# Top-64 attention: two of the seven removals of found candidates go from VectorE to GpSimd, whose mask of a row is issued in six parts

## The reference, cut to what matters

```python
scores = einsum('bhqd,bhkd->bhqk', q, k) / scale       # [16 heads, 2048, 1601 or 2048]
top_scores, top_idx = jax.lax.top_k(scores, 64)
w = softmax(top_scores)                                # all other keys have weight 0
out = einsum('bhqk,bhqkd->bhqd', w, v gathered by top_idx)
```

## Time and profile before

| | us |
|---|---|
| median of 3 runs | 8678.82 (8678.73 to 8685.87) |
| the profiled execution: its own time | 8695.39 |
| its span, first to last instruction | 8693.6 |
| busy in the span: TensorE, VectorE, ScalarE, GpSimd | 6502.8, 6476.1, 4444.7, 3965.1 |

### The profile page before, as it was taken

The page is one execution under the profiler, slowest core; times in us unless marked ns, Lnnn a source line. Parts: engine busy times, 40 slices in busy tenths (PEclk is TensorE's granted clock), DMA queues, the critical chain, the costliest instruction groups (busy, mean ns, idle before and its releaser), DMA issues. The chain is left out here.

```text
span 8693.6 us, 157925 instructions
## 1 busy us (share of the span) xinstructions
PE 6502.8 (75%) x31114; PEld 2666.4 (31%) x31240; DVE 6476.1 (74%) x41675; ACT 4444.7 (51%) x8491; POOL 3965.1 (46%) x2643
## 2 busy tenths in 40 slices
PE   6998477774677767998566777776657899999974
PEld 3333222221222224665222232222223322222213
DVE  4664899999999994554799999999996444444424
ACT  1665466664666652112567777776655332323320
POOL 0001355553555541221456666665644065656650
PEclk7999666665666667999677777776767999999986
DMA  2000000000000000000000000000000411111122
GB/s 75 19 22 12 31 8 5 8 5 4 8 5 8 8 2 17 22 15 16 32 9 5 7 8 9 6 9 5 6 5 19 164 31 31 38 40 31 31 47 64
DMA packets 81575, 193.10 MB, mean 22 GB/s; under 512 B 23728, under 2 KB 38062, under 8 KB 77230
## 3 DMA queue, kind: packets, MB, share of 16 engines
q1 hardware_dynamic: 72366, 169.98, 7.0%
q10 hardware_dynamic: 8192, 12.59, 0.6%
HBM read 118.97 MB, written 62.76 MB: 21 GB/s over the span
## 5 line engine op out<-in xcount | busy, mean ns | idle before, releaser
L2152 DVE TENSOR_REDUCE l1xc_part_max<-l1xc_by_query 128x1 f32<-128x512 f32 (+1 forms) x1024 | 559.5, 571 | 753.3 <-PE l1xc_by_query L2011 731.4
L2110 ACT ACTIVATE l1xc_prob<-l1xc_less_max 128x512 f32<-128x512 f32 (+1 forms) x832 | 451.2, 594 | 1004.4 <-PE l1xc_less_max L2025 935.9
L582 PE MATMUL l1ac_by_query<-l1ac_k_stack,l1ac_q_stack 97*128 (+1 forms) x1024 | 423.0, 470 | 695.8 <-ACT keep_xT L677 364.2
L770 DVE MAX8 l1ac_cand<-l1ac_score 128x8 f32<-128x39 f32 (+1 forms) x6656 | 863.1, 192 | 31.8 <-ACT l1ac_score L677 17.0
L552 POOL TENSOR_SCALAR l1ac_lost<-l1ac_score,l1ac_tops 128x2048 bf16<-128x2048 f32 x128 | 696.0, 5437 | 411.4 <-DVE l1ac_tops L789 387.1
L582 PE MATMUL l0xc_by_query<-l0xc_k_stack,l0xc_q_stack 97*128 (+2 forms) x1024 | 375.1, 431 | 664.8 <-ACT keep_xT L677 448.7
L770 DVE MAX8 l1ac_cand<-keep_xT 128x8 f32<-128x39 f32 (+1 forms) x6656 | 863.0, 191 | 4.4
L1973 POOL TENSOR_TENSOR l1xc_total<-l1xc_total,l1xc_prob 128x2048 f32<-128x2048 f32 (+1 forms) x176 | 794.2, 4513 | 72.3 <-POOL l1xc_v_tile L1983 72.0
L770 DVE MAX8 l0xc_cand<-l0xc_score 128x8 f32<-128x31 f32 (+1 forms) x6656 | 800.9, 182 | 27.6 <-ACT l0xc_score L677 15.8
L552 POOL TENSOR_SCALAR l1ac_lost<-keep_xT,l1ac_tops 128x2048 bf16<-128x2048 f32 x128 | 696.3, 5440 | 244.4 <-DVE l1ac_tops L789 244.4
L770 DVE MAX8 l0xc_cand<-keep_xT 128x8 f32<-128x31 f32 (+1 forms) x6656 | 801.7, 182 | 4.4
(11 more groups left out here) (479 smaller groups left out, 14320.9 us busy)
## 6 DMA issues: line engine op xcount, KB each, us to landing
l1xc_k<-wide_k SPq DMA_DIRECT2D x32, 400.2 KB
moe_w<-in_L_ffn_mlp_w_dram SPq DMA_DIRECT2D x16, 512.0 KB, 4.2
wide_q<-l1xp_full SPq DMA_DIRECT2D x8, 1024.0 KB, 3.9
...
```

The source lines that it names most:

```text
L582: nc.tensor.matmul(sA[c % 2][:, 0:w], Qm[0:SHIFT_ROW, bass.ds(at + i * P, P)], Kb[0:SHIFT_ROW, bass.ds(at + a, w)], start=True, stop=True) ...
L770: seg = nc.vector.max(new[:, j:8 * NSEG:NSEG], score[i % 4][:, a:a + w])
L2110: nc.scalar.activation(prob[0:n, buf(j), c], yP[c % 2][0:n], ACT.Exp).then_inc(y_taken, 1)
L2152: nc.vector.tensor_reduce(part_max[:, i % 2, c:c + 1], a_bank(i, c)[:, 0:w], AX.X, ALU.max).then_inc(a_taken, 1)
```

## The change

VectorE's first two removals of a tile are dropped. In their place GpSimd runs two instructions each, in `remove`: TENSOR_SCALAR over 52 candidates (is it at least the eighth value found, times -3e38) into a new tile `gone`, and TENSOR_TENSOR, which adds `gone` to the candidates. VectorE's first two MAX8 count up `picked`, GpSimd waits for it, and VectorE's second and third MAX8 wait for `removed`. The 52 segment instructions are spread anew: 15 of them stand behind the first MAX8 and 15 behind the second (`GAP` is 9 places), and one or two behind each of the 11 steps that are left. GpSimd's mask is issued in six parts (267 or 342 keys each), of which one stands behind each removal and the rest behind `part_max` and `stage_v`. In slot s GpSimd removes from row tile s-2 while it masks row tile s-3.

```diff
--- before.py
+++ after.py
@@ -362,6 +362,8 @@
     SET = 3
     BEGIN = 7
     TURN = 3
+    POOLED = 2
+    MASK_PARTS = tiles_of(nk, (nk + 5) // 6)
     QUADS = [list(range(a, min(a + 4, NKT))) for a in range(0, 16, 4)]
     UNITS = QC * NKT
     DV = DH + 1
@@ -377,6 +379,7 @@
         cands = [s.sb(f"cand{b}", [P, 8 * NSEG]) for b in range(2)]
         tops = s.sb("tops", [P, 8, TOPK])
         top_full = s.sb("top_full", [P, TOPK])
+        gone = s.sb("gone", [P, NSEG])
         missed, missed2 = s.sb("missed", [P, 4]), s.sb("missed2", [P, 4])
         anyflag = s.sb("anyflag", [1, 4])
         less_exact = s.sb("less_exact", [P, 1])
...
@@ -546,22 +550,45 @@
                 hold(pool, (parted, at + 5))
                 nc.gpsimd.tensor_copy(stat_parts[:, 2], neg_rest[:, 1]).then_inc(parted, 1)
 
-            def mask(n, i, chunk):
-
-                hold(pool, (y_formed, NKT * (chunk - 1) + F_AHEAD))
-                nc.gpsimd.tensor_scalar(lost[:, i % 8, 0:nk], score[i % 4][:, 0:nk], tops[:, i % 8, TOPK - 1:TOPK], None,
-                                        ALU.is_lt).then_inc(masked, 1)
+            def mask(i, k):
+
+                a, w = MASK_PARTS[k]
+                part = nc.gpsimd.tensor_scalar(lost[:, i % 8, a:a + w], score[i % 4][:, a:a + w],
+                                               tops[:, i % 8, TOPK - 1:TOPK], None, ALU.is_lt)
+                if k == len(MASK_PARTS) - 1:
+                    part.then_inc(masked, 1)
+
+            def remove(n, i, r):
+
+                part = cands[i % 2][:, 0:UPTO[r]]
+                hold(pool, (picked, POOLED * n + r + 1))
+                nc.gpsimd.tensor_scalar(gone[:, 0:UPTO[r]], part, tops[:, i % 8, 8 * r + 7:8 * r + 8], -3.0e38,
+                                        ALU.is_ge, ALU.mult).then_inc(goes, 1)
+                hold(pool, (goes, POOLED * n + r + 1))
+                nc.gpsimd.tensor_tensor(part, part, gone[:, 0:UPTO[r]], ALU.add).then_inc(removed, 1)
+
+            def picks(h, i):
+
+                return (not (isinstance(h, int) and h == 0) or i >= 2) and not (isinstance(h, int) and h == H and i >= 2)
 
             def slot(h, i, searching, producing):
+                settling = settles(h, i)
+                it = (i - SET) % QT
+                ht = h if i >= SET else h - 1
+                todo = list(range(len(MASK_PARTS))) if settling else []
+                if settling:
+                    hold(pool, (extracted, h * QT + i - SET + 1), (y_formed, NKT * (4 * ht + it // 4 - 1) + F_AHEAD))
+                if picks(h, i):
+                    for r in range(POOLED):
+                        remove(h * QT + i - 2, (i - 2) % QT, r)
+                        for k in todo[r:r + 1]:
+                            mask(it, k)
+                if settling and it % 4 == 3:
+                    part_max(ht, it // 4)
                 if producing:
                     stage_v(*products_of(h, i))
-                if settles(h, i):
-                    n, it = h * QT + i - SET, (i - SET) % QT
-                    ht = h if i >= SET else h - 1
-                    hold(pool, (extracted, n + 1))
-                    if it % 4 == 3:
-                        part_max(ht, it // 4)
-                    mask(n, it, 4 * ht + it // 4)
+                for k in todo[POOLED if picks(h, i) else 0:]:
+                    mask(it, k)
 
             pool.sem_inc(masked, S_AHEAD)
             slots(pool, slot)
@@ -759,7 +786,8 @@
                 top = tops[:, (i - 1) % 8]
                 count, other = chains[i % 2], chains[(i + 1) % 2]
                 first = isinstance(n, int) and n == 0
-                SLICES = 2 * ROUNDS + 1
+                GAP = 9
+                SLICES = 2 * ROUNDS + 1 + POOLED * (GAP - 2)
                 searching = not (isinstance(n, int) and n == H * QT)
 
                 def some_segments(r):
@@ -780,21 +808,36 @@
                 dve.wait_ge(count, 1)
                 some_segments(0)
                 at = 1
+                place = 1
                 for r in range(2 * ROUNDS - 1):
                     some = top[:, 8 * (r // 2):8 * (r // 2) + 8]
                     part = old[:, 0:UPTO[r // 2]]
+                    last = r == 2 * ROUNDS - 2
+                    if r < 2 * POOLED:
+                        if r % 2 == 0:
+                            if r:
+                                hold(dve, (removed, POOLED * (n - 1) + r // 2))
+                            else:
+                                dve.wait_ge(count, at)
+                            nc.vector.max(some, part).then_inc(picked, 1)
+                            for _ in range(GAP):
+                                some_segments(place)
+                                place += 1
+                        continue
+                    if r == 2 * POOLED:
+                        hold(dve, (removed, POOLED * n))
                     dve.wait_ge(count, at)
-                    last = r == 2 * ROUNDS - 2
                     if r % 2 == 0:
                         ins = nc.vector.max(some, part)
                     else:
                         ins = nc.vector.match_replace(part, some, part, -3.0e38)
                     ins.then_inc(extracted if last else count, 1)
                     at += 1
-                    some_segments(r + 1)
+                    some_segments(place)
+                    place += 1
                     if r == CHECK_AFTER and i2 is not None:
                         check(n - 2, i2)
-                some_segments(2 * ROUNDS)
+                some_segments(place)
                 dve.sem_clear(count)
 
             CHECK_AFTER = 12
```

More of the change, by code:

```diff
@@ L397, in attend_top @@
          comb_taken, extracted, counted, squared, any_formed, any_taken, masked, checked, parted, st_turned, st_out,
-         st_loaded, passed, full_chain) = (s.sem(x) for x in (
+         st_loaded, passed, full_chain, picked, goes, removed) = (s.sem(x) for x in (
              "ready", "rows_set", "loaded", "a_formed", "a_taken", "y_formed", "y_taken", "staged", "pv_done",
              "o_taken", "comb_formed", "comb_taken", "extracted", "counted", "squared", "any_formed", "any_taken",
-             "masked", "checked", "parted", "st_turned", "st_out", "st_loaded", "passed", "full_chain"))
+             "masked", "checked", "parted", "st_turned", "st_out", "st_loaded", "passed", "full_chain",
+             "picked", "goes", "removed"))
         chains = [s.sem("chain0"), s.sem("chain1")]
```

## The result

The changed kernel takes 9207.65 us (median of 4 runs, 9205.49 to 9215.26); the kernel before took 8682.35 in the same comparison (8678.73 to 8695.11). The ratio is 1.0604, with a 95% interval of 1.0585 to 1.0622: 525 us slower. The direction was forecast; the size was not. The forecast was +315 us, 8995, and the range ended at 9160.

The account below looks back on a forecast made before the run. VectorE was taken to set the pace, with ScalarE's flag chain nearly as late. Rounds growing 2.60 and 2.17 us, times 64, give +166 and +139, full searches +10: +315 us, 8995 us, range 8820 to 9160.

Parts of the forecast that it names:

- the wait for the second removal: VectorE ahead of its third MAX8: a slot may start 0.40 us late for nothing, so no cost in undisturbed tiles.
- The loop: GpSimd's slot 2 mask end, ScalarE's slot 3, slot 0's flag, VectorE's load, next slot 2: 36.41 us (`l0xc`), 37.52 (`l1ac`).
- flag in slot 0: ScalarE's flag, for which VectorE's load of step 13 waits, ends 6.25 us into slot 0.
- tile 1: VectorE's undisturbed tile, first MAX8 to first MAX8: 8.15 us in `l0xc`, 8.58 in `l1ac`.
- The forecast's base: Round time before the change, loop turn taken off: 33.81 us in `l0xc`, 35.35 in `l1ac`.
- slot 2 of GpSimd: From tile 2's start to GpSimd's mask end, with removals, six parts, `stage_v`, `part_max`: 9.38 us in `l0xc`, 10.48 in `l1ac`.
- the bare load: VectorE's `value_load` and branch at the flag check, covered by one segment instead of three: 0.15 us a tile.
- The first wait: VectorE in tile 3 waits for slot 3's removals on GpSimd: 0.83 us in `l0xc`, about 1.4 in `l1ac`.
- Signs: VectorE: a third of the MATCH_REPLACE8 over 52, busy about 86%; GpSimd's busy time up some 2.4 us a tile.
- VectorE stays the clock: Rival: GpSimd's delay is absorbed and the kernel gets faster, 8607 us, down to 8505; chance 0.08.
- Only the first wait counts: Rival: VectorE's wait for GpSimd's removals costs, ScalarE's flag does not; 8679 us, chance 0.05.
- The heavier case of the loop: Rival: the loop holds but GpSimd is slower yet, removals 0.95 us, fixed part 0.20; 9180 us, over 9160 chance 0.08.

Follow-up runs that it names:

- e5: The changed kernel plus one more GpSimd TENSOR_SCALAR over 267 keys in each slot 2, written to a tile nobody reads: 9331.31 us.
- e6: The changed kernel plus one more GpSimd TENSOR_SCALAR over 267 keys in each slot 1, not slot 2: 9248.48 us.
- e7: The changed kernel with GpSimd's mask whole behind both removals and VectorE's flag check moved behind its last step: 8909.42 us.
- e2: The changed kernel with GpSimd's mask in one instruction, behind both removals, `part_max` and `stage_v`: 9096.85 us.
- e9: The kernel before, all removals on VectorE and GpSimd untouched, with only VectorE's segments spread as in the changed kernel: 8867.56 us.
- e10: The kernel before with GpSimd removing in slots 3, 0 and 1 only, mask whole behind both removals, flag check behind the last step: 8632.78 us.
- e1: The kernel before with GpSimd's mask in six parts and no removal moved: 8772.33 us.

## Why the prediction was right in direction and short in size

Where VectorE and ScalarE would wait, and in `l0xc` the way of the loop, were right. Two terms of the sum failed: GpSimd's slot 2, forecast at 9.38 us and measured at 10.63, and VectorE's undisturbed tile, forecast at 8.15 and measured at 8.70. Within the second, the step that failed is the wait for the second removal, put at nothing and measured at 0.36. In `l1ac` the path was wrong too.

**The loop.** Right in `l0xc`. From the mask's end in slot 2 to the same a round later, with measured values for the forecast's seven: 0.17, slot 3 10.04 (10.04), flag in slot 0 5.84 in the median (6.25), to the load 0.78 (0.78), rest of tile 0 1.64 (1.64), tile 1 8.71 (8.15), slot 2 10.63 (9.38). That makes 37.81 against the table's 37.84. Five terms hold or came out shorter; two were mis-sized, by 1.81 us together, and they carry the error. The flag, 0.41 shorter than forecast, hid a part of it by luck. The forecast's base was also a little high, 33.81 and 35.35 where the medians give 33.69 and 35.02. A sum of this kind comes out wherever each link follows the last one without a pause, so it is no proof by itself. That the links matter is shown by e5 against e6 for GpSimd's slot 2, and for the flag by VectorE's idle time at the load in tiles 3 and 0 and by e7 against e2.

**The term "slot 2 of GpSimd", 9.38, was 1.25 us too small.** Three parts of it. Two removals: 0.93 us each start to start (1908.35 to 1909.28), not 0.78, because TENSOR_SCALAR over 52 with two operations takes 476 ns; I had taken 0.35, with 0.48 as the bad end. That is 0.30. Six parts, start to start: 0.95 + 1.03 + 3.76 = 5.74, not 5.14, mostly since a further instruction costs 0.25 and not 0.17; 0.60. `part_max` and `stage_v`: 1912.19 to 1914.82 is 2.63, not 2.26, because the copy of V stands between two waits now; 0.37. I had made a fixed part of 0.20 the bad end; it measured worse than that. By the factor of two in GPSIMD Engine Reference of the Trainium skill, section Engine selection, the estimate for a removal was 0.48 us; the trace disagrees, with 0.93. Against VectorE's own removal, 0.17, that is a factor of 5 at this size.

**The term "tile 1", 8.15 and 8.58, was 0.56 and 0.73 us too small.** The forecast took 0.20 for the thinner spread (0.05 for single segments, 0.15 at the bare load). e9 measures the spread alone at 0.42 us a tile. The wait for the second removal, which the forecast put at nothing, comes on top. It had 0.40 us of spare for a slot that starts late, but by its own terms every slot starts 0.42 late, behind `picked`: 0.42 + 1.56 + 0.86 + 0.13 = 2.97 against a third MAX8 at 3.0 leaves 0.03. With a removal of 0.93 and a part of 0.95 between, the second removal ends at 1910.89 + 0.29 = 1911.18, 3.23 us after the tile's first MAX8, and the third MAX8 starts 0.15 later, at 3.38; without the wait it would have started at 3.02. So every tile paid 0.36 in `l0xc`. From start to start, in 92 undisturbed tiles of `l0xc`: 8.30 - 0.34 for the two removals + 0.27 at the bare load + 0.36 for the wait + some 0.1 at the thin places = 8.70, as measured. The forecast's sign was thus wrong: it had the undisturbed tile 0.15 us shorter than before, and it became 0.40 longer.

**In `l1ac` the loop closes another way.** The forecast had it pass through slot 3 and slot 0's flag. The medians say: mask end to search 0.17, flag of slot 3 itself 6.62, load 0.80, rest of tile 3 1.70, tiles 0 and 1 9.19 + 9.31, and slot 2, whose mask ends 2.50 - 0.17 us after tile 3 begins, 9.02 + 2.33 = 11.35. Sum 39.14, against 39.15. The way through slot 0's flag is shorter here, as slot 3 of ScalarE takes only 9.11 us. The loads say the same: in tile 3 every one waits about 0.8 or 1.1 us for the flag of slot 3, while in tile 0 the median idle time is 0.21, no more than the bare load's. In tile 1 the flag is often a little late as well: in the rows above, slot 1's search stood 1.86 us for GpSimd's mask of slot 0, its flag ended at 5323.33, and the load followed 0.78 later. No run separates the two ways in `l1ac`. That GpSimd's slot 1 counts there too is shown by e6.

**The first wait.** Forecast 0.83 and about 1.4 us in tile 3; 1.55 and 1.81 here, mostly by the later end of slot 2, and another 0.3 at the third MAX8. The idle time at the load, forecast 1.2 to 1.6, is 0.98 and 1.10 in the rows of `l0xc`: the tiles had become longer, and hid more of the flag. In tile 0 of `l1ac`, where it was forecast too, the flag brings none. Slot 3 begins 2.11 and 2.5 us after tile 3's first MAX8, where 1.4 and 2 were forecast.

**Signs.** The removals over 52 candidates fell to a third, VectorE's share to 85 and 87% (86 forecast), both as said. GpSimd's busy time grew by more than the 2.4 us a tile: from 4.84 to 7.59 in `l0xc` and from 5.93 to 8.66 in `l1ac`, over the whole tiles inside the windows of the earlier trace rows, so 2.7.

**The rivals.** "VectorE stays the clock" falls, its busy share says so; but it comes true in e10, when the removals leave slot 2 alone. "Only the first wait counts" falls by VectorE's idle time at the load, 0.8 to 1.3 us in tile 3 of both blocks and 0.5 to 1.0 in tile 0 of `l0xc`, and by e7 against e2. The heavier case of the loop, 9180, was nearest, but for its reasons only in part. It was right on the removal (0.95, measured 0.93) and nearly so on the fixed part (0.20, measured 0.25). The way was 0.20 us (1908.15 to 1908.35) and not 0.4, the bare load 0.27 and not 0.6, slot 3 in `l1ac` 9.11 and not 10.22, and the wait at the third MAX8 was not in it. That it came near is luck for the larger part. TensorE's granted clock did fall a little, from 0.65 to 0.63 and from 0.73 to 0.70 in the windows, but slot 3 took no longer in `l0xc` (10.04).

**What the parts cost by themselves.** Spread alone +176 us (e9), six parts alone +84 (e1); if these added up, the remaining 265 of the 525 would come with the removals on GpSimd, after the 174 us of VectorE's work that they save. As e7 shows that such parts overlap, this split is an estimate.
